# Recommendation tower on one Trainium2 core: the one-hots of a table made by one comparison with two inputs instead of eight or ten with one

## What is computed

```
e = stack([tbl_f[ids[:, f]] for f in range(26)], axis=1)           # 2048 x 26 x 128
combined = concatenate((dense[:, None, :], e), axis=1)             # 2048 x 27 x 128
inter = einsum('bfd,bgd->bfg', combined, combined)                 # pairs above the diagonal: 351
h = concatenate([dense, inter[:, iu, ju], dense], axis=1)          # 607
h = maximum(h @ W_top1 + b_top1, 0)                                # 512
h = maximum(h @ W_top2 + b_top2, 0)                                # 256
y = h @ W_top3                                                     # 1
```

## Time and profile before

| What | Before |
|---|---|
| median of three runs | 399.78 us (398.67 to 400.17) |
| profiled execution, its span | 400.18 us, 398.4 us |
| PE busy, share of the span | 388.1 us, 97% |
| DVE busy | 245.2 us, 62% |
| ACT busy | 224.5 us, 56% |
| POOL busy | 276.4 us, 69% |
| one-hot comparisons (line 438) | 528 instructions, 164.8 us busy, 383 ns mean |
| gathers (line 297) | 288 instructions, 275.6 us busy, 957 ns mean |
| chain of work that ended last | PE 95%, ACT 3%, DVE 1%, issue 1% |

### The profile page before, as it was taken

How to read it: one execution, slowest core, us unless ns; L and a number is a source line. 1 busy time by engine, 2 the same in 40 slices (tenths; PEclk the granted TensorE clock), 3 DMA queues, 4 the chain that set the end, 5 groups by cost and what they waited for, 6 DMA issues and landing times.

```text
span 398.4 us, 8467 instructions
## 1 busy us (share of the span) xinstructions
PE 388.1 (97%) x3264; PEld 374.7 (94%) x3264; DVE 245.2 (62%) x683; ACT 224.5 (56%) x473; POOL 276.4 (69%) x296
## 2 busy tenths in 40 slices
PE   6998999999999999999999999999999999999997
PEld 5787899999999999999999999999999999999896
DVE  7699859573774947476594847659385756913421
ACT  3455576456573645567375546637554664747462
POOL 5777777777777777777777777777777777776000
PEclk9999999999999999999999999999999999999999
DMA  8995733233333324334232422433233222221000
GB/s 181 251 259 138 170 81 88 77 86 81 74 84 80 77 72 85 78 73 94 73 82 68 85 81 79 88 75 79 71 84 87 54 55 59 56 54 48 2 2 0
DMA packets 24595, 33.98 MB, mean 85 GB/s; under 512 B 8589, under 2 KB 18341, under 8 KB 24556
## 3 DMA queue, kind: packets, MB, share of 16 engines
q0 software_dynamic: 9216, 18.89, 19.3%
q1 hardware_dynamic: 13260, 14.41, 15.0%
q10 hardware_dynamic: 2080, 0.15, 0.5%
HBM read 33.41 MB, written 0.01 MB: 84 GB/s over the span
## 4 chain that ended last, share of the span: by engine, by line
PE 95%; ACT 3%; DVE 1%; issue 1%; DVEq 0%
PE side L561 29%; PE prod L591 27%; PE mlp L609 10%; PE side L572 8%; PE mlp L620 6%; PE side L556 4%; PE mlp L611 3%; PE mlp L628 2%; PE prod L541 2%; PE mlp L601 1%; ACT feats L325 1%; ACT diag L340 1%; PE prod L680 1%; DVE onehot L438 1%; PE side L687 1%
## 5 line engine op out<-in xcount | busy, mean ns | idle before, releaser
L297 POOL DMA_INDIRECT rows<-in_tbl,ids x288 | 275.6, 957 | 89.2 <-issue 85.4
L438 DVE TENSOR_SCALAR onehot<-wanted,row_no 125x256 fp32r<-125x256 int32 (+1 forms) x528 | 164.8, 383 | 17.8 <-PE side L561 13.0
L340 ACT ACTIVATE diag<-prod 27x216 f32<-27x216 f32 x256 | 87.4, 342 | 136.7 <-PE prod L591 133.3
L561 PE MATMUL side<-onehot,table_hi 125*128 125x256 f32 x496 | 126.2, 293 | 0.9 <-issue 0.9
L591 PE MATMUL prod<-feats 128*123 128x108 f32 x1024 | 119.8, 271 | 2.0 <-ACT feats L325 2.0
L561 PE MATMUL side<-onehot,table_lo 125*128 125x256 f32 x496 | 121.1, 283 | 0.0
L591 PEld LDWEIGHTS prod<-feats 128*123 128x123 f32 x1024 | 115.3, 188 | 2.8 <-ACT feats L325 2.6
L466 DVE TENSOR_SCALAR h<-mlp,b_sb 128x128 f32<-128x128 f32 x86 | 24.9, 345 | 118.0 <-PE mlp L611 73.9
L561 PEld LDWEIGHTS side<-onehot,table_hi 125*128 125x128 f32 x496 | 94.7, 191 | 1.7 <-issue 1.7
L561 PEld LDWEIGHTS side<-onehot,table_lo 125*128 125x128 f32 x496 | 95.0, 192 | 0.0
L325 ACT ACTIVATE feats<-side 128x512 f32<-128x512 f32 (+1 forms) x80 | 78.3, 1020 | 1.1
(11 more groups left out here) (49 smaller groups left out, 135.3 us busy)
## 6 DMA issues: line engine op xcount, KB each, us to landing
wanted<-in_small_ids SPq DMA_DIRECT2D x56, 128.0 KB, 3.3
rows<-in_tbl,ids POOLq DMA_INDIRECT x288
feats<-in_tbl SPq DMA_DIRECT2D x7, 448.0 KB
dense<-in_dense_rows SPq DMA_DIRECT2D x16, 64.0 KB, 3.2
w_sb<-in_w_pairs SPq DMA_DIRECT2D x1, 702.0 KB
table<-in_tbl SPq DMA_DIRECT2D x1, 560.0 KB
w_sb<-in_w SPq DMA_DIRECT2D x1, 512.0 KB
feats<-in_tbl SPq DMA_DIRECT2D x7, 52.0 KB
```

The source lines that it names most:

```text
L297: gp.indirect_dma_start(rows[:, q % SLOTS_OF_ROWS, f * D:(f + 1) * D], None, large_tables[g + f], bass.IndirectOffsetOnAxis(ap=ids[:, t, g ...
L340: last = nc.scalar.activation(diag[t % 2][W * i:W * i + SLOTS, s * SEG_GROUPS * SLOTS:(s + 1) * SEG_GROUPS * SLOTS], prod_part(prod[s % 2] ...
L438: made = nc.vector.tensor_scalar(onehot[v % 2][:, c - row_nos_at(h), :], wants, row_no[:, c:c + 1], None, ALU.is_equal)
L561: last = nc.tensor.matmul(look_bank(v)[:, 0:BS], part_of(part, k)[:, c * D:(c + 1) * D], onehot[v % 2][:, c, :], start=(c == 0 and part is ...
```

## The change

In `one_hot`, the loop over the chunks with one `tensor_scalar` each is replaced by one `tensor_tensor` over all chunks. Its first input is the ids of the 256 samples, repeated for each chunk (step 0 over the chunks); its second is the h columns of row numbers, each repeated for 256 samples (step 0 over the samples). The output, the semaphores, and the order of everything else stay.

```
--- before.py
+++ after.py
@@ -434,10 +434,10 @@
                 if v >= 2:
                     dve.wait_ge(look_full, v - 1)
                 h = CH[v % NS]
-                for c in range(row_nos_at(h), row_nos_at(h) + h):
-                    made = nc.vector.tensor_scalar(onehot[v % 2][:, c - row_nos_at(h), :], wants,
-                                                   row_no[:, c:c + 1], None, ALU.is_equal)
-                made.then_inc(onehot_ready, 1)
+                nos = row_no[:, row_nos_at(h):row_nos_at(h) + h]
+                nc.vector.tensor_tensor(onehot[v % 2][:, 0:h, :], wants.rearrange("p (o n) -> p o n", o=1).broadcast_to([CP, h, BS]),
+                                        nos.rearrange("p (c o) -> p c o", o=1).broadcast_to([CP, h, BS]), ALU.is_equal)\
+                    .then_inc(onehot_ready, 1)
```

## The result

The changed kernel takes 492.33 us (median of four runs, 490.29 to 494.48), the kernel before, run four times beside it, 399.70. The ratio is 1.232, 95% interval 1.230 to 1.235. The profiled execution took 494.48 us for a span of 492.7 us.

What follows compares the result with a forecast made beforehand. PE (97% busy) and POOL's gathers were taken as nearly level, POOL having 5.1 us of slack. Span 398.4 - 5.1 + 100 of holds = 493.3 us, plus 1.8 for the profiled execution: 495; range 450 to 530 (8 in 10).

Steps and rivals of the forecast that it cites:

- PE and POOL nearly level, 5.1 us of slack: Per tile POOL's gathers need 22.5 us, PE 23.05; POOL delays beyond 5.1 us in all lengthen the kernel one for one.
- the constant 393.3: Span in us, 398.4 - 5.1, of a kernel where PE waits for the last gather and nothing before it is delayed.
- 2.28 and 2.81 us per comparison: Time on DVE of each new two-input comparison: 56 of 2048 elements at 2.28 us, 8 of 2560 at 2.81.
- the rival of half rate: Mixed types or zero steps run DVE's comparisons at half rate, 4.42 us each; time 639 us, chance 0.03.
- The hold rule: A gather starting during a two-input DVE instruction waits until 0.12 us before its end; one already under way is untouched.
- rival "no hold": DVE's repeated second operand doesn't hold POOL's gathers, which keep their 1.25 us step; time about 399.6 us, chance 0.10.
- 100 us of holds: Delay of POOL's gathers: 56 x 1.54 + 8 x 2.07 = 102.8 us, less 2.5 for back-to-back pairs in the head.
- lock at its best (0.91) or worst (2.16): Phase of DVE's comparisons against gathers locks: least hold gives 457.6 us, chance 0.07 for phase locked; greatest hold 537.6.
- DVE's gain is worth nothing: DVE gets back about 19 us in all, worth nothing after the head and at most 0.9 us in it.
- The clock: PE's granted clock should stay 1.00; if new pauses lowered it, the time would lie above the range.
- The signs named beforehand: In the changed profile: gathers' mean 1.29 us, last gather ending near 466 us, PE's longest wait at the transposes.

Runs made afterwards that it cites:

- two_banks_psum: Changed kernel with lookups and transposes rotating over two PSUM banks instead of three, and row numbers in the idle third bank instead of SBUF; 445.22 us.
- eighth: Against the kernel before: one two-input comparison per chunk (256 elements), eight or ten per table; 417.21 us, ratio 1.045.
- quarter: Against the kernel before: two-input comparisons of 2 chunks each (512 elements), four or five per table; 408.89 us, ratio 1.023.
- one_input: Against the changed kernel: one comparison per table with one tensor input and one scalar per partition, the first chunk's row numbers serving all chunks; 441.33 us.
- half: Against the kernel before: each table's one-hots by two two-input comparisons of 4 or 5 chunks each; 431.40 us, ratio 1.081.

## Why the prediction was right

495 us were forecast, 492.3 measured; the profiled execution, against which the sum was made, took 494.5 where the sum gave 495.1. Part of that nearness is luck: the last gather ended 97.2 us later and not 100, and behind it stood 2.2 us that the sum did not have (1.3 for the landing, 0.9 for the clock).

- **PE and POOL nearly level, 5.1 us of slack.** Right. It is the constant 393.3 of the table, met by seven kernels within 2.1 us.
- **2.28 and 2.81 us per comparison.** Right: 2.288 and 2.836 us. Repeated operands and int32 against fp32 cost nothing; the rival of half rate falls.
- **The hold rule.** Right, and now shown and not only read: two_banks_psum takes away one of the two SBUF inputs and nothing else, and the holds are gone. It is incomplete for runs of short instructions, where seven gathers in eighth and quarter were held over several. The rival "no hold" is refuted by every comparison of the changed trace.
- **100 us of holds.** Gathers are busy for 97.8 us more, or 1.53 us per comparison against 100 / 64 = 1.56. Over the 56 comparisons of 2048 elements the holds have a mean of 1.47 us (forecast 1.54), over the eight of 2560 one of 2.11 (forecast 2.07). The phase did not lock at its best (0.91) or worst (2.16): holds of 0.95, 1.21 and 2.12 us stand side by side in the stretch above. It does lock inside a back-to-back run, which the sums for quarter and eighth missed. That the mean over the kernel came so near is partly luck of mixed phases.
- **DVE's gain is worth nothing.** Right: 14.9 us less busy (19 forecast), none of it in the time.
- **The clock.** Wrong, though it cost little. "Should stay 1.00": it was 0.93 in the mean. The stretch from 202 to 218, in which PE waits 4.43 us for gathers, has PE busy for 11.56 of 16.00 us and the clock at 0.79; before, PE was busy for all of a stretch of 46.10 us at 1.00. The prediction said that a lowered clock would put the time above its range, and that did not happen either. PE is busy for 418.8 us, 85%, where I had forecast 79%. Of its 30.7 us more, only the 0.9 at the end lies on the path; the rest must have filled time in which PE would have waited for POOL, since the sum of 492.7 above has no room for it.
- **The signs named beforehand.** Mean of a gather 1.29 us (1.297 measured), last gather near 466 (463.6), longest wait at the transposes (65.9 us): all there.

On the Trainium skill, page SBUF — State Buffer, section "Who interferes with whom": its rule that DVE with two SBUF inputs contends with a GpSimd instruction that reads SBUF agrees with these traces in both directions (97.8 us more with it, 959 ns per gather without). Its inference that DMAs issued from GpSimd are spared by tensor_tensor does not hold for these gathers. The same section says that DVE's two-port modes, which tensor_scalar can enter, contend with GpSimd, and that whichever of the two issued first has the ports for its whole instruction. The holds at the start in one_input agree with that; the 27 gathers that were under way first and were stopped all the same do not. No run here shows in which mode the instruction ran, or which port it is.

## What to carry to other kernels

When gathers are issued from GpSimd, look at the distance between their starts, not at GpSimd's busy share: at 69% busy it had 5 us to spare in 400. A long DVE instruction with two SBUF inputs costs such a queue, on average, its own length less 0.12 and less half of a gather's step (here 1.47 us for one of 2.29); one operand in PSUM costs it nothing. Short instructions cost less at equal DVE work, but not nothing: 12 us here with 512 elements and 21 with 256, against 98. Fewer instructions on an engine that is idle anyway are no gain, and what they hold may be another engine's path.

## What was not expected of the hardware

- One comparison with one tensor input over 2048 elements took 1.33 us, against 2.28 with two, and held gathers more than two-input instructions of 1.22 us did: 45.3 us more busy than before, against 35.7 in half. It stops gathers at their start and, in their first 0.45 us, under way; the two-input form stopped none of the 42 that were under way in the changed kernel.
- Of two kinds of work that repeat (a gather each 1.25 us, a comparison each 0.60 or 0.34), a hold sets the phase of the first by the second: quarter had 42 such holds, eighth 105.
- A gather can be held over a whole run of short comparisons: six in eighth made 10.7 of its 21.0 us, so that 256-element comparisons cost more than 512-element ones (12.1 us).
- A PSUM operand did not lengthen the comparison: 2281 against 2288 ns.
- A wait of 4.4 us on PE was followed by lookups with matmuls of 0.41 us instead of 0.28, at the lower of the two clock levels (1.2 GHz, not 2.4).
